# Four weight-matrix units of a mixture-of-experts kernel: matrix added by VectorE instead of by identity products

## The chip, the cores and the metric

The kernel runs on one core of a Trainium2 chip. A core has TensorE (matmuls into the accumulation memory PSUM), VectorE, ScalarE, GpSimd, and SyncE, which here only issues DMAs. The metric is the device time of one execution in microseconds (us); 1 us is 0.08% of the kernel.

## The reference

A decoder layer over 4 sequences of 1024 rows, width 256, in float32, with a layer normalisation after each part. The last part has eight experts of hidden width 512, and each weight matrix has a low-rank companion:

```python
def _lora_out(g, W, b, A, B):
    base = jnp.einsum('teh,edh->ted', g, W)
    low = jnp.einsum('ter,edr->ted', jnp.einsum('teh,erh->ter', g, A), B)
    return base + low + b
...
x = _layernorm(x + _L0_attn_ref(x, ...))            # self-attention, 16 heads
x = _layernorm(x + _L0_xattn_ref(x, ctx_768, ...))  # cross-attention
...
scores = jax.nn.softmax(xf @ Wg.T, axis=-1)
expert_weights, expert_indices = jax.lax.top_k(scores, K)   # K = 2 of 8
...
h1 = _lora_in(xf, W1, b1, A1, B1)
h3 = _lora_in(xf, W3, b3, A3, B3)
g = jax.nn.silu(h1) * h3
y_e = _lora_out(g, W2, b2, A2, B2)
y = jnp.einsum('te,ted->td', gates, y_e)
```

## The kernel before

The kernel folds each low-rank pair into its matrix once (W + B A) and then works with full matrices. It has stages: projections, self-attention, cross-attention (`cross_block`, 8 chunks of 512 rows), and the experts (`experts`). The stages are written as separate instruction streams of each engine with semaphores between them; there is no barrier, so an engine goes on to the next stage as soon as its own waits allow. The order within an engine is the order in which the code stands.

During cross-attention each row picks its two experts. VectorE works out the place of each row in a list sorted by expert (`find_places`), and GpSimd scatters the row there in DRAM (`scatter_rows`, line 1176, two scatters for each 128 rows). When all 8 chunks are ranked, VectorE makes tables of 71 tiles of 128 rows (`tabulate`, lines 1121 to 1157): the expert of each tile, and the rows in it. In the middle of that it needs one small TensorE product (line 1525). The semaphore `tables_made` goes to 1 when the experts of the tiles are known, and to 2 at the end.

The output matrices W2 of the eight experts lie in an SBUF tensor `big` as the plain matrices, loaded by SyncE (`load_w2`, line 1308). The low-rank part is put in by eight units (`low_rank2`, two experts and half a matrix each). A unit works in one half of PSUM tensor `ps_l` (`cb_l` in the trace, two banks, used in turn). TensorE multiplies the plain matrix by an identity matrix (line 1446), so that it stands in PSUM, and adds the product of the low-rank factors (line 1452); ScalarE copies the sum back over the plain matrix (`copy_w2`, line 1553) and counts `late_copied`. Unit u waits for the copy of unit u - 2, whose half of PSUM it takes. TensorE has units 2 and 3 before the small product of the tables and units 4 to 7 behind it:

```python
ranks(NCH - 1)
low_rank2(2)
low_rank2(3)
pe.wait_ge(verdict, 2)
nc.tensor.matmul(bank("verdict", NCH, 0)[:, P:P + TABLES * NT], ...)
for u in range(4, 8):
    low_rank2(u)
```

Behind these stands a fallback (`exact_attention`) that each engine skips by a branch, and then `experts`. For tile s, GpSimd gathers the 128 rows (line 2489), once `tables_made` is 2 and all scatters have landed; SyncE moves the tile's W1 and W3 within SBUF to one of three slots (line 2474, two DMAs of 512 KB); TensorE transposes the rows (`turn_x`, line 2535), ScalarE copies them (line 2575), TensorE makes the hidden layer (`hidden`, line 2546), VectorE adds the biases (line 2618), ScalarE applies SiLU (line 2579), VectorE multiplies (line 2627), TensorE applies W2 (`out`, line 2556), VectorE and ScalarE scale the result (lines 2636 and 2585), and GpSimd adds it to the output in DRAM with a scatter (line 2500). Each such scatter waits for the landing of the one before. TensorE's order is turn_x(0), hidden(0), turn_x(1), a wait for `late_copied` of 8, and then for each s: hidden(s+1), turn_x(s+2), out(s). SyncE waits for the rows of tile 0 before it issues the weights of tile 2. At the end SyncE loads the finished rows and they are normalised.

Of the kernel before, what the change touches and what calls it, by code (L numbers as in the profile page):

```python
# [12 lines left out]
ALU = mybir.AluOpType  # L13
# [5 lines left out]
B, S, D = 4, 1024, 256  # L19
# [941 lines left out]
def low_pairs():  # L961

    return [(w, k, q, i) for w in range(2) for k in range(KT) for q in range(2) for i in range(2)]
# [7 lines left out]
def w2_pairs():  # L971

    return [(q, i, m) for q, i in ((1, 0), (0, 0), (0, 1), (1, 1)) for m in range(2)]
# [213 lines left out]
def cross_block(nc, io, cc, sa, ro, x2_all, big, stage, block):  # L1187


    with ExitStack() as ctx:  # L1190
# [3 lines left out]
        def sem(name):  # L1194
            return ctx.enter_context(nc.semaphore("cb_" + name))
# [5 lines left out]
        w13, w2 = (views["w1"], views["w3"]), views["w2"]  # L1201
# [9 lines left out]
        f2, scratch = late.take(P, 2, 3 * D), late.take(P, 6 * D)  # L1211
# [11 lines left out]
        ps_l = [ctx.enter_context(nc.psum_tensor(f"cb_l{i}", [P, 2, 512], F32)) for i in range(2)]  # L1223
        ps_att = [ctx.enter_context(nc.psum_tensor(f"cb_att{i}", [P, 512], F32)) for i in range(2)]

        def low_bank(u, r):
            return ps_att[r][:, :] if u % 3 == 2 else ps_l[u % 3][:, r, :]
# [15 lines left out]
        late_filled, dummies_stored = (sem(n) for n in ("late_filled", "dummies_stored"))  # L1243
        late_copied = ro["late_copied"]
        chosen, placed, weighed, weights_exp = (ro[n] for n in ("chosen", "placed", "weighed", "weights_exp"))

        def bank(kind, n, part):

            return ps_misc[misc[kind, n, part] % 2]
# [71 lines left out]
        def _(pe):  # L1321
# [113 lines left out]
            def low_rank2(u):  # L1435
                q, i, m = w2_pairs()[u]
                if u < 2:
                    pe.wait_ge(exp_done, LOW_A + PAIRS * NCH - 1 + u)
                else:
                    pe.wait_ge(late_copied, u - 1)  # L1440
                if u // 2 % 2 == 0:
                    pe.wait_ge(f2_loaded, 16 * (u // 4 + 2))
                else:
                    pe.wait_ge(ro["w2_loaded"], 16 * (u // 4 + 1))
                for r in range(2):
                    nc.tensor.matmul(ps_l[u % 2][:, r, :], ident[:, :], w2[:, 4 * q + 2 * i + r, 2 * m:2 * m + 2, :],
                                     start=True, stop=False)
                for mm in range(2):
                    for r in range(2):
                        rows = slice(32 * (2 * i + r), 32 * (2 * i + r) + 32)  # L1450
                        a = (2 * m + mm) * P
                        last = nc.tensor.matmul(ps_l[u % 2][:, r, mm * D:(mm + 1) * D], f2[rows, q, a:a + P],
                                                f2[rows, q, 2 * D:3 * D], start=False, stop=(mm == 1))
                last.then_inc(late_filled, 1)

            low_rank(0)
# [14 lines left out]
            for n in range(NCH):  # L1471
# [34 lines left out]
                if n + 1 < NCH:  # L1506
# [3 lines left out]
                turn_outputs(n, (2, 3))  # L1510
            ranks(NCH - 2)
            low_rank2(0)
            low_rank2(1)
            turn_x2(NCH - 1)
            gate(NCH - 1)
# [4 lines left out]
                             start=True, stop=True).then_inc(misc_filled, 1)  # L1520
# [4 lines that stand above are left out]
            nc.tensor.matmul(bank("verdict", NCH, 0)[:, P:P + TABLES * NT], ones[0:NT, :], diagonal_of(scratch),  # L1525
                             start=True, stop=True).then_inc(misc_filled, 1)
# [4 lines left out]
        def _(act):  # L1531
# [18 lines left out]
            def copy_w2(u):  # L1550
                q, i, m = w2_pairs()[u]
                act.wait_ge(late_filled, u + 1)
                nc.scalar.activation(w2[:, 4 * q + 2 * i:4 * q + 2 * i + 2, 2 * m:2 * m + 2, :].rearrange("p r m c -> p r (m c)"),
                                     ps_l[u % 2][:, :, :], ACT.Copy).then_inc(late_copied, 1)
# [36 lines left out]
            def exp_gap(c):  # L1591
                act.wait_ge(weighed, c + 1)
                nc.scalar.activation(ro["e"][:, :], ro["gap"][:, :], ACT.Exp).then_inc(weights_exp, 1)
# [22 lines left out]
            copy_w2(0)  # L1616
            copy_x2(NCH - 1)
            exp_gap(NCH - 1)
            for u in range(1, 8):
                copy_w2(u)  # L1620

        @block.vector
        def _(dve):
# [130 lines left out]
            def make_tables():  # L1754
                def release(instruction):
                    instruction.then_inc(drained("rank", NCH - 1, 0), 1)
                    wait_drained(dve, "rank", NCH - 1, 0)

                def spread(instruction):
                    instruction.then_inc(verdict, 1)  # L1760
                    dve.wait_ge(misc_filled, len(misc) + 1)
                    return table_of(bank("verdict", NCH, 0))

                def known(instruction):
                    instruction.then_inc(ro["tables_made"], 1)

                tabulate(nc, release, step, spread, known, ident, ro, bank("rank", NCH - 1, 0), scratch)

            def copy_low(u):
                w, k, q, i = low_pairs()[u]  # L1770
                for r in range(2):
                    dve.wait_ge(l_filled, 2 * u + r + 1)
                    nc.vector.tensor_copy(w13[w][:, 4 * q + 2 * i + r, k, :], low_bank(u, r)).then_inc(low_copied, 1)

            copy_low(1)
            add_projection(0, 0)
            add_projection(0, 1)
            last1 = statistics1(0)
            moments1(0, last1)
            copy_low(7)  # L1780
            for i in range(2):
                dve.wait_ge(sa["o_stored"][i], 16 * NSTEP // JT // 2)
            normalise_masked(0)
            for u in (10, 12, 13, 15):
                copy_low(u)
# [57 lines left out]
            place_rows(NCH - 1)  # L1843
            make_tables()
            dve.sem_inc(ro["tables_made"], 1)

        @block.gpsimd
        def _(pool):
# [838 lines left out]
def decoder_layer(nc, io):  # L2687
# [15 lines left out]
    with ExitStack() as outer:  # L2703
        cc = cross_constants(nc, outer)
        block = outer.enter_context(nc.Block())
        with ExitStack() as attention:
            sa = attention_space(nc, attention)
            with ExitStack() as early:
                cs = cross_setup_space(nc, early)
                front(nc, io, cc, cs, sa, block)  # L2710
            self_attention(nc, io, cc, sa, block)

        with ExitStack() as late:
            x2_all = late.enter_context(nc.sbuf_tensor("x2_all", [P, NTT, ROW], F32))
            ro = routing_space(nc, late)
            ro |= {n: late.enter_context(nc.semaphore(n)) for n in ("chosen", "placed", "weighed", "weights_exp", "x2_stored",
                                                                    "late_copied", "tables_made", "flag_set", "w13_added", "w2_loaded")}
            ro["x2_all"] = x2_all
            ro["scattered"] = [late.enter_context(nc.semaphore(f"scattered{i}")) for i in range(2)]
            with ExitStack() as inner:  # L2720
                big = inner.enter_context(nc.sbuf_tensor("big", [P, 4 * WSIZE], F32))
                stage = inner.enter_context(nc.sbuf_tensor("stage", [P, KT * HID], F32))
                cross_block(nc, io, cc, sa, ro, x2_all, big, stage, block)
                exact_attention(nc, io, cc, ro, x2_all, big, block)
                experts(nc, io, cc, ro, x2_all, big, stage, block)
# [75 lines left out]
```

## Time and profile before

| | before |
|---|---|
| median of 3 runs | 1248.8 us (1245.96 to 1255.19) |
| profiled execution | 1265.7 us, span 1263.9 us |
| TensorE matmul busy | 1185.1 us, 94% of the span |
| VectorE busy | 852.9 us, 67% |
| ScalarE busy | 790.0 us, 63% |
| GpSimd busy | 773.2 us, 61% |
| TensorE clock granted, mean | 0.982 |

The profiled execution is 16.9 us longer than the median of the others, so that its times serve for differences and not as the time of a run. Busy times are of the whole span; the change touches only some 20 us of it, which start at 820 us.

### The profile page before, as it was taken

To read this page: it belongs to the slowest core of one execution; us is meant where nothing else is said; L and a number is where in the kernel's file an instruction comes from. 1 tells how busy PE (TensorE), PEld (TensorE's weight loads), DVE (VectorE), ACT (ScalarE), POOL (GpSimd) and SP (SyncE) were. 2 spreads that over 40 slices of the span, in tenths; PEclk is the share of its full clock that TensorE was granted. 3 is DMA by queue.
4 is the path that set the end of the run, shared out by engine and by line. 5 is a ranking of instruction groups with operands and counts; after the bars stand their busy time and mean duration, and the time that the engine had idled before them with its cause. 6 is when DMAs were issued, how large, how long until landed. Compare 5 with 4: busy or idle time off the path is not lost.

```text
span 1263.9 us, 28342 instructions
## 1 busy us (share of the span) xinstructions
PE 1185.1 (94%) x10786; PEld 685.3 (54%) x10786; DVE 852.9 (67%) x1548; ACT 790.0 (63%) x952; POOL 773.2 (61%) x512
## 2 busy tenths in 40 slices
PE   7999999999999999999999898689999999999991
PEld 3554233333333333333444443369999999999981
DVE  4456998999899989998468787614445545554551
ACT  4556999999999999998566566122223333232221
POOL 2235788888788888777366977524445455445542
PEclk9999999999999999999999999789999999999996
DMA  7697855595559454462477953657787888887863
GB/s 240 221 339 249 250 89 88 86 273 89 80 97 259 78 77 77 82 131 80 126 182 175 220 175 125 221 210 235 231 256 248 267 263 245 277 263 238 254 198 66
DMA packets 134081, 232.53 MB, mean 184 GB/s; under 512 B 31466, under 2 KB 80399, under 8 KB 133623
## 3 DMA queue, kind: packets, MB, share of 16 engines
q1 hardware_dynamic: 108456, 184.09, 50.1%
q0 software_dynamic: 20864, 35.61, 14.6%
q10 hardware_dynamic: 4622, 10.96, 2.7%
q8 instruction: 90, 1.47, 0.5%
q14 instruction: 49, 0.39, 0.1%
HBM read 103.88 MB, written 52.79 MB: 124 GB/s over the span
## 4 chain that ended last, share of the span: by engine, by line
PE 65%; DVE 17%; issue 6%; DMA 5%; ACT 4%; POOL 2%; another core or an unknown queue 1%; ACTq 0%; SPq 0%; DVEq 0%; POOLq 0%
PE xp_ps_h L2546 18%; PE sa_sum L715 9%; PE sa_o L729 9%; PE xp_ps_y L2556 8%; DVE sa_probs L769 8%; PE qp_ps L319 4%; PE sa_factor L715 4%; DMA y_sum<-stage,xp_place_of 4%; PE qp_ps L346 2%; ACT sa_probs L795 2%; DVE sa_o_out L747 1%; PE cb_misc L1349 1%; PE xp_ps_x L2535 1%; PE cb_misc L1329 1%; PE cb_l L1365 1%
## 5 line engine op out<-in xcount | busy, mean ns | idle before, releaser
L769 DVE TENSOR_TENSOR sa_probs<-sa_sum,sa_strips 128x1024 f32<-128x1024 f32 x352 | 413.2, 1219 | 41.6 <-PE sa_sum L715 40.8
L819 POOL TENSOR_TENSOR sa_probs<-sa_probs,sa_factors 128x1024 f32<-128x1024 f32 x160 | 383.6, 2398 | 92.3 <-ACT sa_probs L789 92.3
L795 ACT ACTIVATE sa_probs<-sa_probs 128x1024 f32<-128x1024 f32 (+1 forms) x256 | 342.7, 1383 | 0.0
L2546 PE MATMUL xp_ps_h<-arena,big 128*128 128x128 f32 x2272 | 267.6, 276 | 5.0 <-ACT arena L2575 3.9
L2546 PEld LDWEIGHTS xp_ps_h<-arena,big 128*128 128x128 f32 x2272 | 265.8, 193 | 11.2 <-ACT arena L2575 5.8
L729 PE MATMUL sa_o<-sa_probs,sa_v 128*17 128x512 f32 x2048 | 264.8, 592 | 0.8 <-POOL sa_probs L819 0.6
L2500 POOL DMA_INDIRECT y_sum<-stage,xp_place_of x71 | 115.0, 1619 | 181.0 <-DMA y_sum<-stage,xp_place_of 56.7
L715 PE MATMUL sa_sum<-sa_qk 97*32 97x512 bf16 x2816 | 200.4, 380 | 11.7 <-DVE sa_probs L769 4.8
L715 PEld LDWEIGHTS sa_sum<-sa_qk 97*32 97x32 bf16 x2816 | 62.9, 95 | 228.7 <-DVE sa_probs L769 130.5
L789 ACT ACTIVATE sa_probs<-sa_factor 128x1024 f32<-128x1024 f32 x160 | 164.2, 1026 | 2.6 <-PE sa_factor L715 1.5
L2585 ACT ACTIVATE stage<-arena,xp_weight_of 128x256 f32<-128x256 f32 x71 | 36.1, 508 | 170.7 <-DVE arena L2636 85.0
L2556 PE MATMUL xp_ps_y<-big,arena 128*128 x568 | 134.5, 380 | 1.3 <-DVE arena L2627 1.3
L2556 PEld LDWEIGHTS xp_ps_y<-big,arena 128*128 128x128 f32 x568 | 102.4, 190 | 12.6 <-issue 1.7
L2489 POOL DMA_INDIRECT arena<-sorted,ro_row_of x71 | 72.9, 1027 | 42.7 <-issue 20.8
L715 PE MATMUL sa_factor<-sa_qk 97*32 97x512 bf16 x1280 | 97.6, 381 | 1.0 <-ACT sa_probs L789 0.7
L2615 DVE CAST xp_place_of<-arena 128x1 uint32<-128x1 f32 x71 | 10.9, 154 | 122.2 <-PE xp_ps_h L2546 100.9
L729 PEld LDWEIGHTS sa_o<-sa_probs,sa_v 128*17 128x17 f32 x2048 | 55.6, 98 | 58.1 <-ACT sa_probs L795 3.6
L586 POOL TENSOR_TENSOR qp_parts<-qp_rest,qp_parts 128x512 bf16<-128x512 f32 x32 | 38.1, 1199 | 79.0 <-ACT qp_parts L390 79.0
L1541 ACT ACTIVATE big<-cb_l,arena 77x1024 f32<-77x1024 f32 x64 | 68.2, 1107 | 29.0 <-PE cb_l L1365 21.6
L2618 DVE TENSOR_TENSOR arena<-xp_ps_h,arena 128x1024 f32<-128x1024 f32 x71 | 86.2, 1215 | 0.0
L2627 DVE TENSOR_TENSOR arena<-arena 128x512 f32<-128x512 f32 x71 | 49.3, 694 | 46.5 <-ACT arena L2579 44.2
L1176 POOL DMA_INDIRECT sorted<-x_all,ro_place_u x64 | 64.7, 1010 | 23.7 <-issue 21.1
(258 smaller groups left out, 1251.8 us busy)
## 6 DMA issues: line engine op xcount, KB each, us to landing
big<-big SPq DMA_DIRECT2D x142, 512.0 KB
sa_qk<-qstack SPq DMA_DIRECT2D x90, 128.0 KB
sa_qk<-kstack SPq DMA_DIRECT2D x90, 128.0 KB
sa_strips<-line SPq DMA_DIRECT2D x3, 3840.0 KB, 18.0
oT<-sa_o_out SPq DMA_DIRECT2D x32, 256.0 KB, 2.4
kstack<-qp_parts SPq DMA_DIRECT2D x48, 128.0 KB, 3.2
qstack<-qp_parts SPq DMA_DIRECT2D x48, 128.0 KB
sa_factors<-factor_line SPq DMA_DIRECT2D x3, 1920.0 KB, 22.1
```

The lines of the kernel that those rows point to most:

```text
L715: last = nc.tensor.matmul(into[c * KEYS:(c + 1) * KEYS, a, :], k[m % 2][:, h, at:at + KEYS], q[m % 2][:, h, ih * CH:(ih + 1) * CH], start= ...
L729: last = nc.tensor.matmul(ps_o[n % 2][32 * h:32 * h + VW, :], v[m % 2][:, jt, VW * h:VW * (h + 1)], probs[s % RING][:, h, :], start=(jt == ...
L769: nc.vector.tensor_tensor(probs[s % RING][:, 2 * half:2 * half + 2, :], ps_sum[sums_before(s, half) % 2][:, :, :], strips[hg % 2][:, 2 * h ...
L789: nc.scalar.activation(probs[s % RING][:, 2:4, :], ps_factor[:, :, :], ACT.Exp, scale=0.25).then_inc(factor_exp, 1)
L795: nc.scalar.activation(probs[s % RING][:, 0:heads, :], probs[s % RING][:, 0:heads, :], ACT.Exp, scale=0.25).then_inc(exp_done, 1)
L819: nc.gpsimd.tensor_tensor(probs[s % RING][:, 2:4, :], probs[s % RING][:, 2:4, :], factors[hg % 2][:, :, c1 - CH:c1][:, :, ::-1], ALU.mult) ...
L1541: nc.scalar.activation(pT[:, first:first + 3:2, :], ps_l[use % 2][:NK, :, :], ACT.Exp, bias=neg_shift[:NK, 0:1], scale=HD ** -0.5).then_in ...
L2489: pool.indirect_dma_start(out=x[s % XRING][:, 0:ROW].bitcast(I32), out_offset=None, in_=io["sorted"], in_offset=bass.IndirectOffsetOnAxis( ...
L2500: pool.indirect_dma_start(out=io["y_sum"], out_offset=bass.IndirectOffsetOnAxis(place_of[:, s:s + 1], 0), in_=y[s % 2][:, :], in_offset=No ...
L2546: last = nc.tensor.matmul(ps_h[parity % 2][:, n, m * P:(m + 1) * P], w_now[s % WRING][:, n, k, m * P:(m + 1) * P], xT[parity % 2][:, k, :] ...
L2556: last = nc.tensor.matmul(ps_y[parity % 2][:, 0:D], g[parity % 2][:, k, :], w2[:, e, k, :], start=(k == 0), stop=(k == KH - 1))
L2618: nc.vector.tensor_tensor(h[i][:, :, :].rearrange("p n (m c) -> p (n m) c", c=P), ps_h[i][:, :, :].rearrange("p n (m c) -> p (n m) c", c=P ...
```

## The change

Units 4 to 7 lose the identity products. Their low-rank products start the accumulation in PSUM themselves, and VectorE, after it has finished the tables, adds the PSUM tile to the plain matrix in SBUF in place (`add_w2`), where ScalarE copied before. Unit 4 and unit 5 wait for the copy of unit 3 as well, so that the count of `late_copied` from two engines keeps its order; units 6 and 7 wait for the additions of units 4 and 5.

```diff
-                    pe.wait_ge(late_copied, u - 1)
+                    pe.wait_ge(late_copied, max(u - 1, 4 if u >= 4 else 0))
...
-                for r in range(2):
+                for r in range(2 if u < 4 else 0):
                     nc.tensor.matmul(ps_l[u % 2][:, r, :], ident[:, :], w2[:, 4 * q + 2 * i + r, 2 * m:2 * m + 2, :],
                                      start=True, stop=False)
...
-                                                f2[rows, q, 2 * D:3 * D], start=False, stop=(mm == 1))
+                                                f2[rows, q, 2 * D:3 * D], start=(u >= 4), stop=(u >= 4 or mm == 1))
...
-            for u in range(1, 8):
+            for u in range(1, 4):
                 copy_w2(u)
...
+            def add_w2(u):
+                q, i, m = w2_pairs()[u]
+                dve.wait_ge(late_filled, u + 1)
+                part = w2[:, 4 * q + 2 * i:4 * q + 2 * i + 2, 2 * m:2 * m + 2, :].rearrange("p r m c -> p r (m c)")
+                nc.vector.tensor_tensor(part, ps_l[u % 2][:, :, :], part, ALU.add).then_inc(late_copied, 1)
...
             make_tables()
             dve.sem_inc(ro["tables_made"], 1)
+            for u in range(4, 8):
+                add_w2(u)
```

## Rows read from the trace of the kernel before

**Rows 1.** Chain that ended last, in order of time; start, length, what.
```profile
820.49 0.63 PE cb_misc L1525 x2
821.12 1.72 PE cb_l L1446 x4
825.81 1.56 PE cb_l L1452 x8
827.39 1.03 ACT big L1553
836.18 0.93 ACT big L1553
```

**Rows 2.** Timeline of TensorE; start, length, instructions, idle time and who ended it.
```profile
822.76 1.13 PE L1452 MATMUL cb_l<-arena 32*128 32x256 f32 x8
823.83 1.98 PE L1446 MATMUL cb_l<-big,arena 128*128 128x512 f32 x4
828.47 3.31 PE L1446 MATMUL cb_l<-big,arena 128*128 128x512 f32 x4 [1.59 <-ACT big L1553]
835.00 1.13 PE L1452 MATMUL cb_l<-arena 32*128 32x256 f32 x8
836.76 0.41 PE L2535 MATMUL xp_ps_x<-arena 128*128 128x128 f32 x2 [0.63 <-issue]
838.33 5.46 PE L2546 MATMUL xp_ps_h<-arena,big 128*128 128x128 f32 x32 [1.16 <-ACT arena L2575]
844.54 3.81 PE L2546 MATMUL xp_ps_h<-arena,big 128*128 128x128 f32 x32 [0.52 <-issue]
```

**Rows 3.** Stretches of time: length, TensorE busy, granted clock, DMA share, GB/s.
```profile
797.72:802.58 4.86, 0.00 (x0) 0.91 0.62 201
802.58:811.32 8.74, 4.17 (x38) 0.50 0.44 154
811.32:815.08 3.76, 3.76 (x12) 0.50 0.60 137
828.99:832.10 3.11, 3.11 (x6) 0.50 0.46 159
839.40:842.70 3.30, 3.30 (x18) 0.51 0.00 0
853.00:1100.00 247.00, 247.00 (x1880) 1.00 0.82 252
```

**Rows 4.** Timeline of SyncE's queue, weights of tiles 0 and 2.
```profile
822.69 1.69 SPq L2474 DMA_DIRECT2D big<-big  x2
832.76 1.15 SPq L2474 DMA_DIRECT2D big<-big  x2
```

**Rows 5.** Timeline of GpSimd: last scatter, first gather.
```profile
824.52 0.96 POOL L1176 DMA_INDIRECT sorted<-x_all,ro_place_u  x1 [0.30 <-issue]
829.83 1.01 POOL L2489 DMA_INDIRECT arena<-sorted,ro_row_of  x1 [4.35 <-DMA sorted<-x_all,ro_place_u]
```

**Rows 6.** Timeline of ScalarE: copies of units 3, 4 and 5.
```profile
819.30 1.02 ACT L1553 ACTIVATE big<-cb_l 128x1024 f32<-128x1024 f32 x1 [1.95 <-issue]
827.39 1.94 ACT L1553 ACTIVATE big<-cb_l 128x1024 f32<-128x1024 f32 x2 [7.06 <-PE cb_l L1452]
```

**Rows 7.** Timeline of VectorE around the end of the tables.
```profile
822.37 0.23 DVE L1157 TENSOR_SCALAR ro_code<-cb_misc 128x71 f32<-128x71 f32 x1
843.84 0.15 DVE L2615 CAST xp_place_of<-arena 128x1 uint32<-128x1 f32 x1 [21.24 <-PE xp_ps_h L2546]
```

**Rows 8.** Line 2618: shortest, median and longest ns, first and last start.
```profile
L2618 DVE TENSOR_TENSOR arena<-xp_ps_h,arena x71: 1212/1215/1217, 844.0 to 1234.3; 128x1024 f32<-128x1024 f32 x71
```

**Rows 9.** Timelines of VectorE and GpSimd, experts.
```profile
850.48 0.69 DVE L2627 TENSOR_TENSOR arena<-arena 128x512 f32<-128x512 f32 x1 [0.57 <-ACT arena L2579]
850.66 1.34 POOL L2489 DMA_INDIRECT arena<-sorted,ro_row_of  x1 [3.60 <-DVE xp_weight_of L2622]
870.65 1.22 DVE L2618 TENSOR_TENSOR arena<-xp_ps_h,arena 128x1024 f32<-128x1024 f32 x1
871.42 1.57 POOL L2500 DMA_INDIRECT y_sum<-stage,xp_place_of  x1 [1.93 <-DVE stage L2616]
```

**Rows 10.** Timeline of GpSimd: output scatters near the end.
```profile
1115.01 1.59 POOL L2500 DMA_INDIRECT y_sum<-stage,xp_place_of  x1 [1.71 <-DVE xp_weight_of L2622]
1123.34 1.58 POOL L2500 DMA_INDIRECT y_sum<-stage,xp_place_of  x1 [5.43 <-DMA y_sum<-stage,xp_place_of]
```

## The prediction

> **What bounds the kernel now.** I read the chain that ended last first, because a saving counts only where that chain runs. It goes through TensorE without a gap around the place of the change: the small product of the tables, then units 4 and 5, ScalarE's copy, units 6 and 7, and a last copy [rows 1]. The timeline of TensorE then shows what follows: it transposes tile 0 at 836.76, waits for ScalarE's copy of it, and runs hidden(0) from 838.33 for 5.46 us, hidden(1) from 844.54 [rows 2]. From 853 to 1100 us it is busy for all of 247.00 us at granted clock 1.00 [rows 3], so tile follows tile and whatever moves the start of hidden(0) moves everything behind it.
>
> The question is thus what else tile 0 needs. The timelines of SyncE and GpSimd tell. SyncE issues the weights of tiles 0 and 1 from 822.69. It issues those of tile 2 at 832.76 [rows 4], and it waits for the rows of tile 0 before that, so these rows are there at 832.76 at the latest. GpSimd starts their gather at 829.83, after 4.35 us idle for the landing of the last scatter, which began at 824.52 [rows 5]. TensorE is the later one by 836.76 - 832.76 = 4.00 us. That is the slack that the change can take, and no more: beyond it, it finds the gather, which hangs on scatters and DMAs that the change leaves alone.
>
> **The change part by part.**
>
> Identity products. One unit has four records of line 1446 in 1.98 us and eight of line 1452 in 1.13 us at full clock [rows 2]. Units 4 to 7 lose the first: 4 x 1.98 = 7.9 us of work at full clock. Unit 6 took 3.31 us for it, since the clock was at 0.50 from 828.99 to 832.10 [rows 2, 3], so 7.9 + 1.3 = 9.2 us leave the chain there, and with them the wait of 1.59 us before unit 6 [rows 2].
>
> Additions. VectorE adds a PSUM tile of 128x1024 to SBUF. The nearest row, line 2618, has the same shape and kinds of operands: 1215 ns, 1212 to 1217 [rows 8]. Four take 4.9 us. VectorE ends the tables at 822.60 and has nothing until 843.84 [rows 7], so they cost it nothing on the path; if hidden(0) came before they end, VectorE would be late for its bias, but that is 12 us away. `tables_made` is counted before the additions, so SyncE and GpSimd do not wait for them. Queued behind each wait of VectorE are only the other additions and then gate(0).
>
> The copies that leave ScalarE, four of about 1.0 us [rows 6], were two on the path: the one of unit 4, and the last one, before the copy of tile 0. ScalarE then does nothing until TensorE has transposed tile 0.
>
> The waits. Unit 4 waits for the copy of unit 3, which ends at 820.32 [rows 6], before the table product ends at 821.12 [rows 1]: no cost. Unit 5 then waits for nothing new. The sum for the units: the chain leaves the table product at 821.12. Unit 4 runs to 822.25 and unit 5 to 823.4 (2 x 1.13). The addition of unit 4 starts at 822.65 and ends at 823.9; unit 6 runs to 825.1, when the addition of unit 5 ends as well; unit 7 runs to 826.3. TensorE is free at about 826.3 in place of 836.13 (835.00 + 1.13), 9.8 us earlier, and the last addition ends at 827.6. W2 is whole before even hidden(0) begins, and out(0) stands behind hidden(1).
>
> What is late next is the gather: 826.3 against 832.76. So 6.4 of the 9.8 us become idle time of TensorE. Only 4.0 us, less one delay, reach the path.
>
> The clock. Here idle time is not free. TensorE stood still from 797.72 to 802.58 and the clock fell within that stretch (mean 0.91); the next unbroken run of work, from 811.32, was at 0.50 for 3.76 us, of a fully busy stretch [rows 3]. In the kernel before, hidden(0) had such a stretch too, 839.40 to 842.70 at 0.51 [rows 3], and that is why it took 5.46 us where hidden(1) took 3.81 [rows 2]. After the change TensorE is idle 6.4 us ahead of tile 0. Bounds for hidden(0): 3.81 us with a full clock throughout, 7.6 us (twice that) with half throughout. I take a half clock for its first 3.9 us, as in the run from 811.32 with a little for the transposes: half of 3.9 is lost, 3.81 + 1.95 = 5.76 us, nearest to the rows that show a rise after steady work. The transposes and copy took 838.33 - 836.76 = 1.57 us; with the clock low I add 0.1.
>
> The sum. Rows of tile 0 at 832.76; hidden(0) starts at 832.76 + 1.67 = 834.43 and ends at 834.43 + 5.76 = 840.19. Before it ended at 838.33 + 5.46 = 843.79. The gain is 3.6 us, 4.0 less 0.1 less 0.3. With the bounds of hidden(0) it is 1.8 us (7.6) to 5.6 us (3.81). Weights of tile 2 are issued at the same 832.76 as before and hidden(2) waits for hidden(1), which ends at 844.54 + 3.81 - 3.6 = 844.8, 12 us later; from tile 3 on the weights are released by hidden(s-3) and move with it.
>
> Does the shift of 3.6 us last to the end? Steady work of tiles hands it on. Late in the stage the output scatters take over: one starts at 1115.01 and the next at 1123.34, 8.33 us later, after 5.43 us idle for a landing [rows 10], and TensorE, which needs about 5.5 us for a tile, begins to wait. But these scatters started from TensorE's results, with the same distance to it, so they move as well. I book the whole 3.6 us, with their scatter in the range.
>
> One rule of the Trainium skill speaks against additions on VectorE at this place. First the row: a gather beside VectorE's line 2627, whose two inputs are both in SBUF, took 1.34 us [rows 9], against 1.01 us for the first one alone [rows 5]. A scatter beside line 2618, with one input in PSUM, took 1.57 us [rows 9], no longer than the 1.59 of another [rows 10]. The additions read one input from PSUM, so I book nothing. The Trainium skill, GPSIMD Engine Reference, section 1 Specifications, says that GpSimd shares its SBUF interfaces with VectorE and contends with VectorE instructions in a two-port mode or with two SBUF inputs; by that rule, too, these additions are the harmless kind, and if they were not, two scatters would be stretched by 0.3 us each, 0.7 us in all, and hide behind the same landing at 829.83.
>
> **The rivals.**
>
> A: VectorE's additions come late. In the kernel before ScalarE's copy of unit 4 should have started at 823.9, when unit 4 had ended (822.76 + 1.13), and started at 827.39 [rows 2, 6], 3.5 us late, while weights were on their way. The same could hit VectorE there. With 3.5 us more, TensorE ends unit 7 at about 829.8 (at half clock for units 6 and 7, 832.1), still ahead of the gather: no loss. If VectorE is held until the weights of tiles 0 and 1 are in, about 829.8, the addition of unit 4 ends at 831.1, unit 6 at half clock (2.3 us) at 833.4, unit 7 at 834.6 to 835.7, and tile 0 starts 1 to 2 us before the old 836.76. The gain is then 1.5 us, the time 1247.3. For it: ScalarE's row. Against: the other copies came at once. The Trainium skill, Runtime: NRT & Kernel Launch, section Instruction fetch mechanics, holds that code is fetched ahead in order and that only a taken branch makes an engine wait for it; ScalarE had no branch between those two copies, so the row stands against reading that rule as a promise, and if it holds for VectorE this rival is void.
>
> B: The clock eats it. TensorE's idle time of 6.4 us leaves it at half clock for all of hidden(0), 7.6 us, and the beginning of hidden(1) (half of 3 us, 1.5 us). The gain is 4.0 - 0.1 - (7.6 - 5.46) - 1.5 = 0.3 us, the time 1248.5. For: sparse work from 802.58 to 811.32, 4.17 us of 8.74, did not raise the clock [rows 3]. Against: the three runs of steady work had it back after 3.1 to 3.8 us [rows 3].
>
> C, slower: The output scatters. From 1123 on the scatters, not TensorE, set the pace, and each waits for the landing of the one before. One long landing costs 8.33 - 5.52 = 2.8 us [rows 10] once there is no reserve. If the other placing of transfers in time gives two more of these in the last 100 us, 5.6 us are lost and 3.6 won: 2 us slower, 1250.8. It decides from two on; with one more the change still gains 0.8. For: the runs of one kernel differ by 9 us. Against: nothing ties the landings to when the stage starts.
>
> D: The change does not do what it says, because the gather was the bound already: then TensorE would have waited for it, and its wait at 836.76 was 0.63 us with nothing named [rows 2]. Time 1248.8.
>
> **How the numbers follow.** Profiled, 1265.7 - 3.6 = 1262.1 us; for the median 1248.8 - 3.6 = 1245.2 us. That the stage is 1.3% faster unprofiled changes 3.6 us by nothing. Chances: forecast 0.58 (gain 1.8 to 5.6: 1243.2 to 1247.0), A 0.12, B 0.12, C 0.12, D 0.03, others 0.03. The range takes in A, B and C and the spread of the runs shown, 2.8 us below the median and 6.4 above: 1240 to 1252 us. A measurement of this kernel can tell about 1% from no change, 12.5 us. No case reaches that: the whole slack is 4.0 us, and all the work removed is 9.2. So within 1%: 0.93; faster by more 0.04, for something the trace hides, such as a gather that comes earlier; slower by more 0.03, four or more long landings.
>
> **What would show it.** Right: units 4 to 7 without line 1446, ending near 826 us; four additions of 1.2 us on VectorE between 822 and 829; TensorE idle some 6 us until the gather lands; transposes of tile 0 near 832.8 on the scale of before; hidden(0) near 5.8 us with a stretch at 0.50; from there rows as before, 3.6 us earlier. Wrong: line 2535 still near 836 (A, or a gather that moved), hidden(0) above 7 us (B), scatters more than 7 us apart oftener behind 1115 us (C), or gathers that move by themselves, since the DMA queues meet other traffic.

## The result and the profile after

The changed kernel is slower: ratio to the kernel before 1.0059, 95% interval 1.0035 to 1.0083. The medians of 20 runs each are 1262.6 us (1248.3 to 1271.3) and 1257.8 us (1246.0 to 1268.8). Two more measurements, on two chips, gave 1.0057 (1.0019 to 1.0094) and 1.0039 (1.0004 to 1.0074). So all three show a loss, 5 to 7 us by the ratios and within 1%. The ratios leave out runs more than 1.5% above the fastest of their kernel, 6 of the 20 before and 2 of the 20 after; over all 20 runs each the medians differ by 4.8 us, the figure used below, and the means by 3.7.

The profiled execution of the changed kernel has a span of 1259.5 us, which is 4.4 us less than the 1263.9 us of the trace of before. One pair of traces thus says "faster" where 20 runs say "slower". It must be read by its parts.

TensorE, timeline; start, length, instructions, idle time before and who ended it:

```profile
814.05 0.63 PE L1525 MATMUL cb_misc<-arena 71*128 71x213 f32 x2
815.15 6.24 PE L1452 MATMUL cb_l<-arena 32*128 32x256 f32 x32 [0.47 <-ACT big L1553]
826.55 0.66 PE L2543 MATMUL xp_ps_x<-arena 128*128 128x128 f32 x2 [5.16 <-DMA arena<-sorted,ro_row_of]
827.69 6.56 PE L2554 MATMUL xp_ps_h<-arena,big 128*128 128x128 f32 x32 [0.47 <-ACT arena L2583]
834.99 3.81 PE L2554 MATMUL xp_ps_h<-arena,big 128*128 128x128 f32 x32 [0.52 <-issue]
```

VectorE, GpSimd and SyncE, timelines:

```profile
815.93 0.23 DVE L1157 TENSOR_SCALAR ro_code<-cb_misc 128x71 f32<-128x71 f32 x1
816.33 1.22 DVE L1773 TENSOR_TENSOR big<-cb_l,big 128x1024 f32<-128x1024 f32 x1 [0.17 <-PE cb_l L1452]
821.44 1.22 DVE L1773 TENSOR_TENSOR big<-cb_l,big 128x1024 f32<-128x1024 f32 x1 [0.48 <-PE cb_l L1452]
...
818.09 0.96 POOL L1176 DMA_INDIRECT sorted<-x_all,ro_place_u  x1 [0.30 <-issue]
823.65 1.01 POOL L2497 DMA_INDIRECT arena<-sorted,ro_row_of  x1 [4.60 <-DMA sorted<-x_all,ro_place_u]
...
826.54 1.15 SPq L2482 DMA_DIRECT2D big<-big  x2
```

Granted clock of TensorE, in stretches (length, TensorE busy, clock, DMA share, GB/s):

```profile
815.20:816.30 1.10, 1.10 (x10) 1.00 0.35 130
816.40:821.40 5.00, 4.99 (x24) 0.50 0.91 350
821.40:826.50 5.10, 0.00 (x0) 0.50 0.52 185
827.70:830.40 2.70, 2.70 (x12) 0.50 0.90 316
844.10:1100.00 255.90, 255.79 (x1943) 1.00 0.82 250
```

Here the local picture is the forecast one. The identity products of units 4 to 7 are gone [rows 2], four additions of 1.22 us stand on VectorE, and TensorE, done at 821.4, waits 5.16 us until the gather has landed. The first gather itself comes at 823.65 instead of 829.83 [rows 5], 6.2 us earlier. The change does nothing to it, so this is a difference of the two executions, not of the kernels. Counted from the first gather, hidden(1) starts after 11.34 us (834.99 - 823.65), against 14.71 before (844.54 - 829.83): 3.4 us gained, for 3.6 forecast. The clock was at 0.50 from 816.40 on, in units 4 to 7, where TensorE was busy for 4.99 of 5.00 us. It fell before the wait of 5.16 us and not in it, was still at 0.50 at the start of hidden(0), and hidden(0) took 6.56 us where I had 5.76.

That makes 9.6 us of lead at hidden(1), and only 4.4 are left at the end. The stage of the experts gave back some 5 us. The timeline of GpSimd shows the output scatters where it begins:

```profile
1016.42 1.58 POOL L2508 DMA_INDIRECT y_sum<-stage,xp_place_of  x1 [1.84 <-DVE stage L2624]
1024.47 1.58 POOL L2508 DMA_INDIRECT y_sum<-stage,xp_place_of  x1 [5.17 <-DMA y_sum<-stage,xp_place_of]
1030.58 1.58 POOL L2508 DMA_INDIRECT y_sum<-stage,xp_place_of  x1 [3.23 <-DMA y_sum<-stage,xp_place_of]
1036.43 1.58 POOL L2508 DMA_INDIRECT y_sum<-stage,xp_place_of  x1 [2.96 <-ACT stage L2593]
...
1060.80 1.57 POOL L2508 DMA_INDIRECT y_sum<-stage,xp_place_of  x1 [1.80 <-DMA y_sum<-stage,xp_place_of]
1070.35 1.58 POOL L2508 DMA_INDIRECT y_sum<-stage,xp_place_of  x1 [6.69 <-ACT stage L2593]
```

The landing of one scatter ends the wait of the next. With a tile every 5.52 us, distances of 8.05, 6.11, 5.85 and 9.55 us put the scatters behind TensorE. Once ScalarE's line 2593, which itself waits for a landing, is the releaser, the scatters set the pace. In the trace of before the long landing of [rows 10] at 1123 us begins this; here it is the one at 1070, while the stage had begun 9.6 us earlier. The chain that ended last is now 15% DMA and 53% PE:

```profile
PE 53%; DVE 16%; DMA 15%; issue 6%; POOL 4%; ACT 4%; SPq 0%; DVEq 0%; ACTq 0%; POOLq 0%
```

Before, it was 65% PE and 5% DMA.

### The profile page after: what moved, and what is told of

It reads as the page before. It is cut to its first block, busy times and chain, and to the rows that moved or that the text cites. A ratio compares the mean times of both kernels' runs of the same rounds, so it can differ in the third digit from the quotient of the medians.

```text
span 1259.5 us, 28310 instructions
## 1 busy us (share of the span) xinstructions
PE 1179.0 (94%) x10770; PEld 683.3 (54%) x10770; DVE 857.0 (68%) x1552; ACT 784.4 (62%) x948; POOL 772.8 (61%) x512
## 4 chain that ended last, share of the span: by engine, by line
PE 53%; DVE 16%; DMA 15%; issue 6%; POOL 4%; ACT 4%; SPq 0%; DVEq 0%; ACTq 0%; POOLq 0%
DMA y_sum<-stage,xp_place_of 13%; PE xp_ps_h L2554 12%; PE sa_sum L715 9%; PE sa_o L729 9%; DVE sa_probs L769 8%; PE xp_ps_y L2564 5%; PE sa_factor L715 4%; PE qp_ps L319 4%; ACT sa_probs L795 2%; PE qp_ps L346 2%; POOL sorted L1176 1%; DVE sa_o_out L747 1%; ACT stage L2593 1%; PE cb_misc L1349 1%; PE cb_misc L1329 1%
```

## The experiments

In what follows, each trace is cut into three distances, all read from the start of instructions in the timelines. **A** goes from SyncE's weights of tile 2 (issued as soon as the rows of tile 0 are there) to the start of hidden(1). **B** goes from there to the start of hidden(70), the last tile; without any wait it is 380.8 us. **C** goes from there to the end.

| trace | A | hidden(0) | B | C | sum | late from tile | over 7 us apart | by ScalarE |
|---|---|---|---|---|---|---|---|---|
| before | 11.8 | 5.46 | 385.8 | 33.6 | 431.1 | 57 | 7 | 19 |
| before (e12) | 5.7 | 3.84 | 388.6 | 33.9 | 428.2 | 50 | 7 | 27 |
| before (e13) | 5.5 | 3.84 | 380.8 | 30.9 | 417.3 | none | 6 | 0 |
| before (e14) | 7.4 | 5.47 | 389.2 | 33.5 | 430.1 | 48 | 7 | 24 |
| changed | 8.4 | 6.56 | 390.4 | 34.1 | 432.9 | 46 | 7 | 31 |
| changed (e1) | 9.8 | 5.95 | 392.8 | 34.8 | 437.4 | 38 | 6 | 37 |
| changed (e7) | 7.3 | 5.18 | 391.6 | 32.6 | 431.4 | 42 | 7 | 26 |
| changed (e17) | 7.3 | 5.25 | 396.1 | 35.2 | 438.5 | 38 | 9 | 35 |

"Late from tile" is the first tile whose hidden layer starts over 0.25 us behind its time without waits. The last two columns count output scatters: those that start more than 7 us after the one before, and those whose wait ScalarE's scaling (line 2585 before, 2593 after) ended. Long distances are as frequent in both kernels. What differs is how soon TensorE falls behind; from there on each tile costs it 0.4 to 0.5 us more.

**The changed kernel again (e1).** No edit.

> The changed kernel as it is, a second time, for its time and for one more trace. Theory (the scatter chain): the experts stage has two paces, about 5.52 us for a tile while TensorE sets it and about 5.95 us once each output scatter waits for the landing of the one before; in the changed kernel the second pace sets in earlier. The ratio to before is then again above 1.003 and the trace shows scatters released by ScalarE's line 2593 from well before the tile at 1120 us. Rival (chance): the 0.6% was a draw of the chip and the day; the ratio is then 0.997, the local gain of 3.6 us.

Measured: ratio 1.0057 (1.0019 to 1.0094), and TensorE falls behind at tile 38, where in the trace of before it was 57: the expectation holds, and the rival (0.997) is out. The trace also shows that the additions do not always run as smoothly as in the first one. TensorE and VectorE:

```profile
828.46 0.23 DVE L1157 TENSOR_SCALAR ro_code<-cb_misc 128x71 f32<-128x71 f32 x1
832.64 2.35 DVE L1773 TENSOR_TENSOR big<-cb_l,big 128x1024 f32<-128x1024 f32 x2 [3.95 <-remote]
...
833.92 3.78 PE L1452 MATMUL cb_l<-arena 32*128 32x256 f32 x16 [4.46 <-DVE big L1773]
840.14 0.66 PE L2543 MATMUL xp_ps_x<-arena 128*128 128x128 f32 x2 [2.44 <-issue]
841.27 5.95 PE L2554 MATMUL xp_ps_h<-arena,big 128*128 128x128 f32 x32 [0.47 <-ACT arena L2583]
```

VectorE stands still for 3.95 us between the tables and the first addition, which the trace puts down to something outside of the core's engines, while the weights are on their way; this is the kind of delay that ScalarE's copy had in [rows 6], now on the other engine. (In e17 the additions were on time, in e7 the second was 2.65 us late.) Units 6 and 7 run at half clock (3.78 us for two), and then TensorE is idle another 2.44 us with nothing named, although the rows were there at 838.16. That idle time stands where TensorE's code branches past the fallback. In the trace of before it was 0.63 [rows 2], in e2 below nothing, and in e10 3.82; no run tests what sets it.

**Identity products kept, results unused (e2).**

```diff
-                for r in range(2 if u < 4 else 0):
+                for r in range(2):
...
-                                     start=True, stop=False)
+                                     start=True, stop=(u >= 4))
```

> As after, but TensorE makes the eight identity products of units 4 to 7 all the same, and the low-rank products then start the accumulation anew and write over them, so TensorE starts the experts when it did before. Theory 1 (the earlier start of TensorE against the rest is what upsets the later chain): the ratio to before is 1.000, within 0.002. Theory 2 (VectorE's additions, or the copies that ScalarE no longer makes, upset it, and the gain of TensorE's time is there): slower than the changed kernel by about 3.6 us, ratio about 1.009. Theory 3 (chance): ratio 1.000, and the changed kernel again is at 0.997.

Measured: 1.0011 (0.9964 to 1.0059), A 11.5, B 380.8, C 31.1. The additions were late here as well (4.86 us after the tables, of which 3.35 after unit 4's products had ended), so A is long. But nothing waited in B. The ratio of theory 2, 1.009, is outside of the interval, and theory 3 asked for 0.997 in e1, which gave 1.0057. Theory 1 fits. But the interval also reaches the 1.0057 of e1, and a single trace without waits says little, since the kernel before has one in four: that the additions have no part in the slow scatters is not shown.

**The serial chain of scatters taken away (e3, e4).** The output leaves out what odd tiles add. From the kernel before and from the changed one:

```diff
-                else:
-                    pool.wait_ge(y_stored[(s - 1) % 2], 16 * ((s - 1) // 2 + 1))
-                pool.indirect_dma_start(out=io["y_sum"], out_offset=bass.IndirectOffsetOnAxis(place_of[:, s:s + 1], 0),
+                elif s >= 2:
+                    pool.wait_ge(y_stored[s % 2], 16 * (s // 2))
+                pool.indirect_dma_start(out=(io["y_sum"], odd_sum)[s % 2], out_offset=bass.IndirectOffsetOnAxis(place_of[:, s:s + 1], 0),
```

> The kernel before with the output scatters of odd tiles sent to another DRAM tensor, so that a scatter waits for the landing of the one two tiles back instead of the last one; the output leaves out what odd tiles add. The transfers stay the same in number and size. Theory (scatter chain sets the pace late in the stage): TensorE no longer waits, the 4.8 us that it waited between 1140 and 1220 us go, and of the five serial scatters at the end (4.55 us each) about half; 1.0 to 1.6% faster, ratio 0.984 to 0.990. Rival (TensorE and the weights are the bound, the chain is only idle time): only the end gets shorter, ratio 0.992 or more.

> The changed kernel with the same edit, again without what odd tiles add. Theory (the chain took the gain back): with the chain out of the way the gain on TensorE shows, so this is 3.6 us faster than the kernel before with the same edit (2 to 5 us), ratio to before 0.981 to 0.987. Rival (the loss is elsewhere, for example in VectorE or in code loading): it stays slower than the kernel before with the same edit by some 7 us.

Measured: 0.9927 (0.9884 to 0.9970) and 0.9920 (0.9883 to 0.9958), medians 1260.9 and 1262.4 us. Both ratios miss the ranges of their theories (0.984 to 0.990 and 0.981 to 0.987). B is 381.3 and 380.8, C 27.5 and 27.4, so the waits are gone in both. The first and the last start of line `hidden` (the row is the line's own: shortest, median and longest ns, first and last start), e3 and e4:

```profile
L2547 PE MATMUL xp_ps_h<-arena,big x2272: 272/275/377, 841.9 to 1231.2; 128*128 128x128 f32 x190
```

```profile
L2555 PE MATMUL xp_ps_h<-arena,big x2272: 272/275/580, 846.0 to 1237.1; 128*128 128x128 f32 x190
```

With the chain gone, the two kernels take the same time within 1.5 us. The intervals, 0.4% to each side, are nearly as wide as the loss, so it is B and C of the traces, equal without the chain and longer with it, that put the loss of the changed kernel in the wait for the scatters. The 3.6 us in favour of the change do not appear either. The stretch from first to last start is 389.3 and 391.1 us, longer by 1.8 in the changed kernel, and the longest matmul took 377 ns in the one and 580 ns in the other: a cold hidden(0), 3.84 against 6.02 us. A is 8.5 and 9.9.

**The code's length given back (e5, e8).** In the first traces TensorE's code loads (the larger instruction queue) came at other distances from the row loads in kernels whose TensorE code is shorter by 32 instructions.

```diff
+                for r in range(2 if u >= 4 else 0):
+                    nc.tensor.matmul(ps_l[u % 2][0:1, r, 0:1], ident[:, 0:1], ident[:, 0:1], start=True, stop=True)
```

> The changed kernel, with eight products of one column and one row in units 4 to 7, thrown away by the real ones behind them, so that TensorE's code is as long as before at next to no time. In the traces so far TensorE's code loads (the larger instruction queue) of the experts stage come at 167.0 and 181.0 us after hidden(1) in the two traces with the longer code, and at 166.7 to 167.5 and 183.5 in the two with the shorter code, and only in the latter did the output scatters fall behind at the row loads at 182.6. Theory (where the code loads fall decides): the loads are back at 181.0, the scatters do not fall behind for long, and the local gain is all that is left, ratio to before 0.996 to 1.000. Rival (the earlier or colder start of TensorE decides, or chance): the ratio stays at 1.005 to 1.006.

> Eight tiny products, the code length of the kernel before, loads some 2 us ahead of the row loads. Theory: ratio 0.997 to 1.001, at least 0.4% faster than the changed kernel on the same chip. Rival: like the changed kernel.

Measured: 0.9993 (0.9956 to 1.0030) and 0.9996 (0.9960 to 1.0033). Beside e8 the changed kernel had 1.0039 (e7). By time, the expectation holds, and the code loads came at 181 us after hidden(1) again. By trace it does not hold: B is 391.0, 384.1 and, in a third trace (e18), 392.1, in two of three with waits as long as in the changed kernel.

**Longer still (e7, e9, e10).** The changed kernel again, and 16 or 32 such products (`range(4)`, `range(8)`).

> The changed kernel once more, as the first of four that differ only in the length of TensorE's code (0, 8, 16 and 32 tiny products in units 4 to 7) on one chip. Its code loads fall 1.0 us behind the row loads that are issued at 182.6 us after hidden(1). Theory (where TensorE's code loads fall against the row loads decides how soon the output scatters fall behind): the slowest of the four, ratio to before 1.004 to 1.008. Rival (chance): the four are alike within 0.3%.

> Sixteen tiny products: 32 instructions more than the kernel before, code loads some 4 us ahead of the row loads. Theory: ratio 0.996 to 1.001. Rival: like the changed kernel.

> Thirty-two tiny products: code loads 6 to 8 us away from the row loads on either side. Theory: ratio 0.996 to 1.001. Rival: like the changed kernel.

Measured: 1.0039 (1.0004 to 1.0074), 1.0054 (1.0010 to 1.0098) and 1.0052 (1.0017 to 1.0087). All three miss: e7 is not the slowest, and away from the supposed collision the other two are slow too. For 32 products the trace shows a large A, 13.6 us, and B only 386.0: the tiny products take 0.5 us in each unit, TensorE stands idle between them, and for 3.82 us before tile 0. For 16 products, in the longest of its executions, A is 11.6 us and B 393.4. So they do not speak cleanly on the code's length.

**The kernel before with shorter code (e6, e15, e16).** Half of the low-rank products of units 4 to 7 is left out, so the low-rank part is missing in one of two blocks of 128 rows of those matrices.

```diff
-                for mm in range(2):
+                for mm in range(2 if u < 4 else 1):
...
-                                                f2[rows, q, 2 * D:3 * D], start=False, stop=(mm == 1))
+                                                f2[rows, q, 2 * D:3 * D], start=False, stop=(mm == 1 or u >= 4))
```

> The kernel before with half of the low-rank products of units 4 to 7 left out (the low-rank part is missing in one of two blocks of 128 rows of those matrices), which takes as many instructions from TensorE's code as the change does, and some 2 us of its work. Identity products and ScalarE's copies stay. Theory (where the code loads fall decides): code loads at 183.5 us after hidden(1), scatters that fall behind there, ratio to before 1.003 to 1.007 in spite of less work. Rival (start or chance): ratio 0.997 to 1.000.

> A second trace of the kernel before with TensorE's code as short as in the changed kernel (half of the low-rank products of units 4 to 7 left out). Hidden(1) to hidden(70) takes 380.8 to 381.3 us where nothing waits. Theory (shorter code makes the output scatters fall behind sooner): 389 us or more, as in all four traces with the short code so far (390.4 to 392.8). Rival (chance): as spread as with the code of the kernel before, 380.8 to 391.0.

> A third trace of the same; theory: 389 us or more, rival 380.8 to 391.0.

Measured: 1.0007 (0.9971 to 1.0043), below what the theory asked, though this kernel also has some 2 us less work. B is 391.1, 380.8 and 390.6: one of the three has no wait at all. The sums of A, B and C, 427.9, 420.9 and 430.8, have the mean 426.5, and the four traces of before 426.7. Shorter code of TensorE alone does not do it every time, and the theory falls in this form. The one trace without waits (e15) has a hidden(0) of 5.47 us, partly at half clock, so that such a start does not bring the waits about by itself either.

**More traces of the kernel before and of the changed one (e12 to e14, e17, e18).** No edit; e18 is the kernel of e5.

> The kernel before, for a second trace of it. The prediction's 3.6 us rest on one trace, in which TensorE was ready 4.00 us after the rows of tile 0. Theory (that trace was a late one, because ScalarE's copy of unit 4 was held up and the clock fell): the distance from the landing of the rows, told by SyncE's weights of tile 2, to the start of hidden(1) is 8.5 to 11.8 us here, against 8.5 to 9.9 in the changed kernel; TensorE waits less than 5 us in all for the output scatters.

> As the look before it, a third trace of the kernel before: rows of tile 0 to hidden(1) 8.5 to 11.8 us; output scatters cost TensorE 0 to 10 us. If all looks of this kernel lie above 9.3 us of such waits, the theory of the code's length falls.

> A fourth trace of the kernel before, with the same expectations as the third.

> A fourth trace of the changed kernel. Theory: hidden(1) to hidden(70) 389 us or more; rival 380.8 to 391.0. Rows of tile 0 to hidden(1): 7 to 10 us, since hidden(0) runs at half clock for a part.

> A third trace of the changed kernel with eight tiny products, so with the code length of before. Theory: anywhere from 380.8 to 391.0, not always high; the rival expects no difference to the others of this call.

Much of this misses. A is 5.7, 5.5 and 7.4 us in e12 to e14, below the expected 8.5, and the waits of e12 are 7.8 us for less than 5 expected. e17 is as the theory expected, and e18 lies 1.1 us above its range. These traces bear on the local gain. TensorE in e13, end of unit 7 and tile 0:

```profile
825.32 1.13 PE L1452 MATMUL cb_l<-arena 32*128 32x256 f32 x8
827.45 0.41 PE L2535 MATMUL xp_ps_x<-arena 128*128 128x128 f32 x2 [0.99 <-DMA arena<-sorted,ro_row_of]
828.34 3.84 PE L2546 MATMUL xp_ps_h<-arena,big 128*128 128x128 f32 x32 [0.47 <-ACT arena L2575]
```

and its clock, in the stretches of the units' end and of hidden(0):

```profile
821.00:828.30 7.30, 5.87 (x26) 1.00 0.50 175
828.30:832.10 3.80, 3.77 (x33) 1.00 0.88 284
```

The kernel before already waits for the gather here, 0.99 us; in e12 it is 1.21 and in e14 1.49 us. There is no slack of 4.00 us to take in these three. The trace of the prediction had it because in that execution ScalarE's copy had been 3.5 us late [rows 6] and the clock had fallen [rows 3]. In the three others ScalarE's copies of units 4 to 7 followed each other every 2.97 us. What the change does bring is idle time of TensorE, and a start of the experts at half clock: hidden(0) took 5.18 to 6.56 us in all four traces of the changed kernel; before, it took 3.84 in two of four and 5.46 or 5.47 in the others. In all four traces of the changed kernel the clock was down before TensorE had ended unit 7. In e12 and e13, with the identity products in place, it stayed at 1.00 from the units to the end of hidden(0). The mean of A is 7.6 us before and 8.2 after, with values that overlap: no gain is seen, and a loss of 0.6 us is not resolved.

The mean of B is 386.1 before and 392.7 after (380.8 to 389.2 against 390.4 to 396.1, 1.2 us between the nearest two), that of C 33.0 and 34.2. The sums differ by 435.1 - 426.7 = 8.4 us, more than the 4.8 us between the medians. Four traces a side are few, and e12 to e14 come from another chip than e1, e7 and e17, so the size of these differences is uncertain; the times were measured side by side.

**Two complete sums (e11).** The changed kernel, the idea of e4 with the whole output: odd tiles go to a second tensor that starts from zeros, and VectorE adds both before the last normalisation.

```diff
+                pool.indirect_dma_start(out=io[("y_sum", "y_odd")[s % 2]], out_offset=bass.IndirectOffsetOnAxis(place_of[:, s:s + 1], 0),
...
+                sp.dma_start(odd[:, :, :], io["y_odd"][chunk_of(c), :].rearrange("(p t) d -> p t d", t=TT)
+                             ).then_inc(rows_loaded[c % 2], 16)
...
+                nc.vector.tensor_tensor(chunk_rows(c), chunk_rows(c), odd[:, :, :], ALU.add).then_inc(joined, 1)
```

> The changed kernel with two complete sums in DRAM: the output scatters of odd tiles go to a second tensor that starts from zeros, SyncE loads both for a chunk of rows, and VectorE adds them before the last normalisation. A scatter then waits for the one two tiles back. Theory (the serial chain of scatters costs 5 to 12 us in the stage and some 6 at the end): 0.3 to 0.7% faster than before, ratio 0.993 to 0.997, less than the 0.8% of the version that left the second sum out, since each chunk has a second load and an addition of 1.2 us, one of them at the end. Rival (the added loads collide with the weights as the row loads do): 0.999 or more.

Measured: 0.9950 (0.9923 to 0.9978), as expected. It is faster than the kernel before, and so than the changed one. B is 380.8, so nothing waits, and C is 30.3, 2.9 more than without the second load.

## Why the prediction was wrong

It said 1245.2 us, 3.6 us less than before; it is 1262.6, 4.8 us more than the kernel before. Of the 17.4 us between the two times, 9.0 are the base: the median of the kernel before is 1257.8 in 20 runs and was 1248.8 in the three shown. The other 8.4 are the effect, 3.6 forecast as won and 4.8 lost.

**"TensorE is the later one by 836.76 - 832.76 = 4.00 us."** This step failed first. It is right for that execution and not for the kernel. In three more traces TensorE was ready first and waited 1.0 to 1.5 us for the rows. This is what rival D says, at 0.03.

**"I book the whole 3.6 us, with their scatter in the range."** This failed with the larger sum. B grew by 6.6 us in the mean of four traces each, and C by 1.2. The place is that of rival C, the output scatters, which I had put at 0.12 and at a net loss of 2 us. Its condition, two more long landings, was not met: scatters more than 7 us apart number 6 or 7 before and 6 to 9 after, so that a hit by rival C would have been luck. What the traces show is that TensorE falls behind sooner, at tiles 38 to 46 for 48, 50, 57 or never before, and then loses 0.4 to 0.5 us on every tile. The argument that the scatters "started from TensorE's results, with the same distance to it, so they move as well" overlooked that they had almost no reserve: the kernel before has traces with B anywhere from 380.8 to 389.2, so the loss was there to grow.

**The additions**: 1.22 us each for 1.22 forecast, at full length beside GpSimd's scatters, as said. They were on time in two traces of four and late in e1 and e7. In e1, with 3.95 us, tile 0 started 2.0 us after the rows, near the price of rival A, but not by its path: the units had ended at 837.70, before the rows, and the rest was TensorE's idle time of 2.44 us.

**The clock**: half clock at the start of hidden(0) came as forecast, but for another reason than the given one. I had it fall while TensorE stood idle ahead of tile 0; in all four traces it was down before that, at the table product or in the first two of the units, and these ran partly at half clock (6.24 us for the 4.5 booked in the first trace). The size was off too: hidden(0) took 5.18 to 6.56 us, for 5.76 forecast. And 5.46 us, what it was compared with, is what two of four traces of before have; the other two have 3.84.

**Units 4 to 7**: 7.9 us of identity products are gone from TensorE and end in idle time, as the step "what is late next is the gather" said.

What stays open is why the changed kernel's scatters fall behind sooner. That the loss is theirs is shown by the traces of e3, e4 and e11, whose B has no waits. The additions of VectorE are neither shown to cause it nor excluded (e2). TensorE's shorter code alone does not always bring it (e6, e15 and e16); the times of e5 and e8 point to the code's length, their traces do not. The earlier start of the experts stage was not tested alone.

## What to carry to other kernels

Before time is taken out of an engine, see in several executions that it is the last one there: one trace of this kernel showed TensorE 4.0 us late at a place where three others showed it early. Look at the clock of the work that is left, not only of the next stage: here it fell in the shortened units. And a serial chain of DMAs that has nearly the same pace as the engine it follows can be the bound in most executions, even if one trace shows no waiting for it: with that chain split, the changed kernel was 0.5% faster than the kernel before, while without the split, and with 7.9 us less of matmuls, it was 0.4 to 0.6% slower.

## What the runs showed of the hardware

An engine can stand still for 3.4 to 4.8 us in the middle of straight code, with its operands ready, while weights are being moved: ScalarE for 3.50 us in [rows 6], VectorE for 3.95 in e1, 3.35 in e2 and 4.76 in e8. No branch stands there, and no run tests the cause. Where TensorE's code branches past the fallback, its idle time with nothing named was 0.63 us in the trace of before, 2.44 in e1, 3.82 in e10 and nothing in e2.

TensorE's clock can fall while it is busy: in the first trace of the changed kernel it went from 1.00 to 0.50 at about 816.4 us, between two stretches in which TensorE was busy for 1.10 of 1.10 and 4.99 of 5.00 us. Ahead of them it had idled 0.47 us.

The landing of the same indirect scatter of 128 rows took 3.6 us at the least, 4.7 in the median and 8.8 at the most within one execution of the changed kernel. Its line's row, microseconds from issue to landing:

```profile
DMA to landing us min/median/max: 3.6/4.7/8.8
```

Without waits the 69 tiles from hidden(1) on take 380.8 us in all of e2, e4, e11, e13 and e15, to 0.1 us. The spread of this stage with one chain, up to 15 us, did not appear with two (e3, e4, e11: 380.8 to 381.3), so it is waiting for landings.
